# First layer of a four-layer kernel: the skip term and gate as five VectorE operations, and GpSimd's fading ahead of its scatters and fetches

## What is computed

```python
xBC = causal_conv_silu(xBC, conv_w)            # xs (512), B (128), C (128)
dt  = softplus(dt_raw + dt_bias); cum = cumsum(dt * A) in each chunk
Yd   = sum over j <= i of (C_i . B_j) * exp(cum_i - cum_j) * dt_j * xs_j
Yoff = exp(cum_i) * C_i . S_before             # S: the state before the chunk
S    = exp(cum_last) * S + sum of wdec * B * xs
y    = Yd + Yoff + D * xs                      # D * xs: the skip term
yz   = y * silu(z)                             # the gate
out  = (yz * rsqrt(mean(yz * yz) + eps) * norm_w) @ W_out.T
```

## Time and profile before

| | us |
|---|---|
| median of 3 runs | 1502.84 |
| lowest, highest | 1494.15, 1506.90 |
| the profiled execution, own time | 1498.83 |
| its span (first to last instruction) | 1497.1 |
| chunk loops of the first layer end, and the second layer starts, about | 587 |

### The profile page before, as it was taken

The page is one execution under the profiler, slowest core; times in us unless marked ns, Lnnn a source line. Parts: engine busy times, 40 slices in busy tenths (PEclk is TensorE's granted clock), DMA queues, the critical chain, the costliest instruction groups (busy, mean ns, idle before and its releaser), DMA issues. The chain is left out here.

```text
span 1497.1 us, 21861 instructions
## 1 busy us (share of the span) xinstructions
PE 1286.0 (86%) x7439; PEld 804.8 (54%) x7443; DVE 885.9 (59%) x1723; ACT 567.9 (38%) x957; POOL 354.7 (24%) x344
## 2 busy tenths in 40 slices
PE   5677988998988687999999998999766989998987
PEld 3334646654664455666666644454543456544564
DVE  5767566556656585543224379889777453556334
ACT  2474476547647551222222242443312313223311
POOL 3186031221302522510301002221037000000045
PEclk9788999999999888999999999999857999999999
DMA  9142123122211412300000150000002100111123
GB/s 360 55 139 84 47 60 96 50 54 71 79 41 35 132 51 97 103 1 0 0 0 0 68 186 0 1 0 1 2 28 85 31 28 29 36 43 57 57 58 111
DMA packets 72082, 88.87 MB, mean 59 GB/s; under 512 B 19174, under 2 KB 55334, under 8 KB 71337
## 3 DMA queue, kind: packets, MB, share of 16 engines
q1 hardware_dynamic: 65836, 70.78, 15.1%
q0 software_dynamic: 6144, 16.79, 3.5%
HBM read 61.14 MB, written 26.38 MB: 58 GB/s over the span
## 5 line engine op out<-in xcount | busy, mean ns | idle before, releaser
L414 PE MATMUL l_banks<-l_xnT,all_region_a 128*128 128x512 f32 x288 | 133.7, 612 | 5.6 <-ACTq L805 4.8
L2019 PE MATMUL l_banks<-l_xnT,mid_region_c 128*128 128x512 f32 (+1 forms) x192 | 89.6, 617 | 10.8 <-DVE l_xnT L2235 10.8
L970 POOL TENSOR_TENSOR all_region_b<-all_region_b,l_lc 128x512 f32<-128x512 f32 x64 | 88.2, 1398 | 31.5 <-DMA all_region_b<-l_lc_rows 31.2
L414 PEld LDWEIGHTS l_banks<-l_xnT,all_region_a 128*128 128x128 f32 x288 | 55.0, 197 | 65.9 <-issue 55.5
L794 ACT ACTIVATE all_region_b<-all_region_b 128x512 f32<-128x512 f32 x64 | 69.5, 1087 | 17.9 <-PE l_banks L414 14.0
L414 PE MATMUL l_banks<-all_region_a,all_xa 128*128 x234 | 68.7, 411 | 6.9 <-DVE all_x L1041 5.4
L1200 DVE SCALAR_TENSOR_TENSOR l_xbc<-l_pre,all_cols,l_xbc 128x512 f32<-128x512 f32 x72 | 61.7, 857 | 19.2 <-ACT l_xbc L727 14.2
L2019 PEld LDWEIGHTS l_banks<-l_xnT,mid_region_c 128*128 128x128 f32 (+1 forms) x192 | 35.2, 189 | 57.3 <-issue 45.4
L962 POOL TENSOR_TENSOR l_yr<-l_yr,all_neg_half 128x1 f32<-128x1 f32 x16 | 10.3, 643 | 232.7 <-DVE l_yr L1063 232.7
L2902 POOL TENSOR_TENSOR l_rstd<-l_moments,all_neg_half 128x4 f32<-128x4 f32 x12 | 12.4, 1032 | 220.8 <-DVE l_moments L2962 220.8
L1257 DVE TENSOR_TENSOR all_region_b<-all_region_b,l_cbd 128x512 f32<-128x512 f32 x64 | 59.0, 924 | 7.6 <-ACT all_region_b L794 3.9
(11 more groups left out here) (475 smaller groups left out, 2854.6 us busy)
## 6 DMA issues: line engine op xcount, KB each, us to landing
all_region_b<-l_lc_rows SPq DMA_DIRECT2D x256, 64.0 KB, 2.0
all_xa<-slots_in SPq DMA_DIRECT2D x39, 128.0 KB, 2.1
slots_out<-all_xa SPq DMA_DIRECT2D x39, 128.0 KB, 2.1
mid_vector_rows<-slots_in SPq DMA_DIRECT2D x39, 128.0 KB, 2.1
slots_out<-all_region_a SPq DMA_DIRECT2D x39, 128.0 KB, 1.7
slots_in<-l_xp SPq DMA_DIRECT2D x4, 1024.0 KB, 12.8
all_region_a<-l_gate_up SPq DMA_DIRECT2D x1, 4096.0 KB, 15.8
all_x<-x SPq DMA_DIRECT2D x4, 512.0 KB, 5.7
```

The lines of the kernel that those rows point to most:

```text
L414: return nc.tensor.matmul(out, lhsT, rhs, start=start, stop=stop, **kw)
L970: nc.gpsimd.tensor_tensor(bc[:, k, :, :], bc[:, k, :, :], spread(lc[:, c, heads], 1, BLK), ALU.subtract).then_inc(dd_ready.sem, 1)
L2019: return nc.tensor.matmul(out, lhsT, rhs, start=start, stop=stop)
```

## The change

The skip matmuls and their diagonal matrix are gone. `assemble` starts the sum in PSUM itself. VectorE's `take_y` forms y + D * xs by four operations of 128 columns (one input in SBUF, one in PSUM, D as a scalar for each partition), waits for them, and gates by a fifth of 512 columns with both inputs in SBUF. ScalarE waits for it before it overwrites `xbc` for the next group. GpSimd's list and loop are new, and three places where VectorE adds the fetched rows and measures.

```diff
         def assemble(g, c):
+            pe.wait_ge(yd_ready.sem, yd_ready.done(g, c))
+            jobs.wait_room(pe, 0, ("y", g, c))
             bank = jobs.bank(("y", g, c))
-            pe.wait_ge(yd_ready.sem, yd_ready.done(g, c))
...
-                    mm(yout[32 * m:32 * m + 32, :, q, :], turn[:, q, :], yd[:, m::4, :], False, False,
+                    mm(yout[32 * m:32 * m + 32, :, q, :], turn[:, q, :], yd[:, m::4, :], q == 0, False,
...
-        def skipped(g, c):
...
-                mm(bank[:, k * P:(k + 1) * P], skip[:, k, :], xbc[:, k, c * P:(c + 1) * P], k == 0, False,
-                   skip_group_check=True)
...
-                    if k == 1:
-                        skipped(g, c)
                     near(g, c, k)
...
                 if j == 0 and g > 0:
                     act.wait_ge(conv_ready.sem, conv_ready.done(g - 1))
+                    act.wait_ge(yg_ready.sem, yg_ready.done(g - 1))
...
-            skips(g)
...
-        late = {0: ((6,), (7, 8)), 1: ((9, 10), (11, 12)), 2: ((13, 14, 15), ())}
+        late = {0: ((4,), (5, 6, 7)), 1: ((), (8, 9, 10, 11)), 2: ((), (12, 13, 14, 15))}
...
             differences(g, 0)
-            if g == 0:
-                for t in range(GT, GT + 2):
-                    scatter(t)
             for c in range(NCH):
+                fade(g, c)
+                ahead, behind = late.get(c, ((), ())) if g == 0 else ((), ())
+                for t in ahead:
+                    scatter(t)
+                if c + 1 < NCH:
+                    differences(g, c + 1)
+                for t in behind:
+                    scatter(t)
                 if (g, c) == (GROUPS - 1, 1):
                     for t in range(GT):
                         fetch(t)
-                fade(g, c)
...
                 if c > 0:
                     out_scale(g, c - 1)
-                for t in behind:
-                    scatter(t)
...
-            nc.vector.tensor_tensor(yg[:, :, :], jobs.bank(("y", g, c)).rearrange("p (k n) -> p k n", k=Z_BLK),
-                                    zs[:, :, c * P:(c + 1) * P], ALU.mult).then_inc(yg_ready.sem, 1)
+            bank = jobs.bank(("y", g, c))
+            for k in range(Z_BLK):
+                nc.vector.scalar_tensor_tensor(
+                    out=yg[:, k, :], in0=xbc[:, k, c * P:(c + 1) * P], scalar=col("D", k),
+                    in1=bank[:, k * P:(k + 1) * P], op0=ALU.mult, op1=ALU.add)
             jobs.free(dve.drain(), ("y", g, c))
+            nc.vector.tensor_tensor(yg[:, :, :], yg[:, :, :], zs[:, :, c * P:(c + 1) * P], ALU.mult).then_inc(
+                yg_ready.sem, 1)
...
                 tiles_and_unit(g, c, 1)
-                if (g, c) == (GROUPS - 1, 1):
-                    add(0)
-                    add(1)
+                if (g, c) == (GROUPS - 1, 2):
+                    add(2)
+                    add(3)
...
                 tiles_and_unit(g, c, 2)
-                if (g, c) == (GROUPS - 1, 1):
-                    add(2)
-                    add(3)
+                if (g, c) == (GROUPS - 1, 2):
+                    measure(0)
...
                     out_stats(g, c - 1)
                 if (g, c) == (GROUPS - 1, 1):
-                    measure(0)
+                    add(0)
+                    add(1)
```

More of the change, by code:

```diff
@@ L174, in layer0 @@
     yr = sb("yr", [P, 2])
-    skip = pre[:, 4, CONV_K - 1:].rearrange("p (k n) -> p k n", k=Z_BLK)
     lmax = sb("lmax", [P, TILES])
@@ L304, in layer0 @@
     yd_ready = Event(sem("l0_yd_ready"), NCH)
-    skip_ready = Event(sem("l0_skip_ready"), 1)
     yg_ready = Event(sem("l0_yg_ready"), NCH)
@@ L587, in assemble @@
             jobs.fill(last, ("y", g, c))
-        def skipped(g, c):
-            if c == 0:
-                pe.wait_ge(skip_ready.sem, skip_ready.done(g))
-            jobs.wait_room(pe, 0, ("y", g, c))
-            bank = jobs.bank(("y", g, c))
-            for k in range(Z_BLK):
-                mm(bank[:, k * P:(k + 1) * P], skip[:, k, :], xbc[:, k, c * P:(c + 1) * P], k == 0, False,
-                   skip_group_check=True)
         def out_proj(g, c):
@@ L766, in conv_silu @@
             nc.scalar.activation(xbc[:, j, :], xbc[:, j, :], ACT.Silu).then_inc(xbc_ready.sem, 1)
-        def skips(g):
-            act.wait_ge(conv_ready.sem, conv_ready.done(g, 4))
-            if g == 0:
-                act.wait_ge(mem.const_ready, mem.n_const)
-            for k in range(Z_BLK):
-                last = nc.scalar.activation(skip[:, k, :], ident[:, :], ACT.Copy, scale=col("D", k))
-            last.then_inc(skip_ready.sem, 1)
         def place(g, c):
@@ L1009, in _ @@
             differences(g, 0)
-            if g == 0:
-                for t in range(GT, GT + 2):
+            for c in range(NCH):
+                fade(g, c)
+                ahead, behind = late.get(c, ((), ())) if g == 0 else ((), ())
+                for t in ahead:
                     scatter(t)
-            for c in range(NCH):
+                if c + 1 < NCH:
+                    differences(g, c + 1)
+                for t in behind:
+                    scatter(t)
                 if (g, c) == (GROUPS - 1, 1):
@@ L1016, in _ @@
                         fetch(t)
-                fade(g, c)
-                ahead, behind = late.get(c, ((), ())) if g == 0 else ((), ())
-                if c + 1 < NCH:
-                    differences(g, c + 1)
-                    for t in ahead:
-                        scatter(t)
                 if c > 0:
                     out_scale(g, c - 1)
-                for t in behind:
-                    scatter(t)
                 if (g, c) == (GROUPS - 1, 2):
```

## The result

The changed kernel takes 1507.2 us (median of 20 runs, 1502.15 to 1512.31); the kernel before, run beside it, takes 1497.95 us (20 runs, 1494.15 to 1506.9). The ratio on record is 1.0052, 95% interval 1.0039 to 1.0064 (the two medians alone give 1.0062): slower, by less than one per cent but by more than chance. The forecast was 1488 us, range 1472 to 1506. The profiled execution has a span of 1503.1 us against 1497.1. The first layer's last chunk hands over to the second layer 3.9 us later, the rest of the program, which is the same code, takes 2.1 us longer. Such a difference says little: over the thirteen profiled executions of this case that rest took between 906.8 and 915.6 us. From here on a chunk runs from one `take_y` to the next, as in the prediction, where nothing else is said.

A forecast was written before the change was run, and what follows sets the result against it. TensorE, busy for 86%, was seen waiting for VectorE, its longest waits leading to GpSimd. Terms 2.6 - 0.8 - 3.5 - 16.9 + 5.4 + 1.2 = -12.0 us gave 1486.8 (1490.8 from the median); forecast 1488, range 1472 to 1506.

The forecast's parts named there:

- Price of the new `take_y`: VectorE, per `take_y`: four operations 1.1 us, gate issued at 1.25, masking of piece 1 done at 5.45; +1.7 us.
- Chunks with tiles: Ten chunks with expert tiles: 1.06 us of matmuls go from each, but the longer `take_y` outweighs it; sum +2.6 us.
- rival (c): Gate held through the fade and four differences, masking 4.1 us later in each of seven chunks: +29, 1516 us; chance 0.12.
- (0, 2) to (0, 3), -3.5 us: Group 0: earlier fade shortens (0, 2), but normalising waits for eight scatters; 4.3 us gained, 0.8 lost to `take_y`.
- (3, 1), -16.9 us: Fade ahead of the fetches ends masking at 511.05 instead of 521.84; adds and measuring move out: -16.9 us.
- (3, 2), +5.4 us: Masking 1.9 us later, one pair of `add` and the measuring come in, small waits go: 26.9 us, +5.4.
- (3, 3) and the tail: (3, 3): bank freed 1.05 us later, skip matmuls gone: 0; layer's end: longer `take_y` in a row of work: +1.2 us.
- ScalarE's copies: Four ScalarE copies at L774 go, some 1.3 us a group: -0.2 us for each group, -0.8 in all.
- the new wait for `yg`: ScalarE's first copy moves by 0.2 us at three group starts, where it waits for TensorE anyway: 0.
- Rival (b): VectorE sets the pace; the 1.7 us pass whole seven times: 11.9 instead of 2.6, 1496 us; chance 0.15.

The follow-up runs named there:

- skip half alone: The changed kernel with GpSimd's order and VectorE's adds and statistics put back as before the change: 1514.79 us, ratio 1.0086 to the kernel before.
- both remedies: The changed kernel with "far" in bank 2 instead of 1 and the gate issued behind `from_state`: 1492.09 us, ratio 0.9948 to the kernel before.
- order-alone kernel: The kernel before with only GpSimd's new order and VectorE's moved adds and statistics, skip term still on TensorE: 1485.24 us, ratio 0.9902.

## Why the prediction was wrong

By its own steps, with the starts of `take_y` in the two profiled executions:

- **Price of the new `take_y`: right.** 1.12 us for 1.1, gate issued at 1.24 for 1.25, masking done at 5.45 as said. The gate took 1.28 or 1.29 us beside a fade in most chunks. The four new operations took 1.12 us also at 534.20, where the fade ran beside them from 534.16.
- **Chunks with tiles, +2.6 us: the step that failed.** The six chunks of groups 1 and 2 that have a `take_y` came out at +1.3, -0.3, +0.4, +1.3, +1.2 and +4.5, together +8.4, where the steps gave +2.6. Each was walked through from `near` on ("TensorE reaches `near` at 382.0 instead of 383.0"). But TensorE comes to `near` only through `far`, and `far` needs the bank that `from_state` frees. In (2, 1) it waited there 1.53 us, so TensorE came no earlier to `near`, and `dn` and the rest behind it moved with it. The prediction knew that bank, but counted it only for (3, 3). In (2, 3) the granted clock also fell to 0.87, from 1.00 before. This term was off by 5.8 us, more than any other; the same wait at `far`, which has no term anywhere in the sum, is also in (0, 3), (3, 2) and (3, 3) below.
- **(0, 1), no term: missed.** 2.6 us longer, the hold of 5.99 us. That is rival (c), in one chunk and not in seven; the 29 us it was priced at didn't come.
- **(0, 2) to (0, 3), -3.5 us: half right.** (0, 2) is 3.0 us shorter and its normalising waits 4.04 us for the scatters, as forecast. But (0, 3) is 1.5 longer, again by `far`: 5.59 us. The step has a slip of its own: eight scatters of 1.23 us from 135.8 end at 145.6, not 146.1. They took longer, too: 11.5 us from the first to the end of the last (138.18 to 149.63).
- **(3, 1), -16.9 us: right, a little too large:** -15.1. Mechanism confirmed by the kernels with and without the fade ahead.
- **(3, 2), +5.4 us: undersized:** +7.5, with 2.75 us at `far` and a clock of 0.82.
- **(3, 3) and the tail, 0 and +1.2:** +2.8 and +1.2. "The bank that `from_state` frees comes 1.05 later and the skip matmuls go: 0" fell on its second half: those matmuls come behind `far`, so that their going can't repay a wait ahead of it, and the wait grew from 3.42 to 4.43.
- **ScalarE's copies, -0.8, and the new wait for `yg`, 0:** the three group starts came out at -1.0, -0.8 and +0.3.

These differences and -0.5 us at the start add up to +3.9 us at the end of the first layer. The prediction had -12.0 there. Seen from the profiled execution, 1486.8 us were forecast and 1504.9 measured: 15.9 us of the miss are these, 2.1 the layers that were not touched. Rival (b) had the right direction for the tile chunks but, for most of it, the wrong reason: with the same work on VectorE, one operation moved or one bank changed took back 12 to 14 us. Its bound of +11.9 for seven chunks still left the total below before, since the rest of the gains was kept. The measured 1507.2 lies just above the range because no rival delayed `far`. The rule of the Trainium skill that was quoted (SBUF — State Buffer, Who interferes with whom) would, as the prediction took it, end the hold of the gate with the one operation that was under way. The row of 5.99 us goes through five, so for this row the measurement decides against that reading; with the 1.29 us of (2, 1) it agrees.

## What to carry to other kernels

An operation that gets longer delays not only what reads its result but every buffer that is freed behind it on its engine: list, for the operations behind it in that queue, which bank or semaphore each frees, and who takes that next, before walking through any chunk. An operation that only makes a result for later (here the gate) belongs behind the one that frees a shared bank, or the two users get banks of their own. The effects of two edits that touch the same wait can't simply be added: removing a long wait can uncover what was hidden beneath it.

## What was not expected of the hardware

- The hold of a VectorE operation with two SBUF inputs came in two forms. Where GpSimd's fade followed its indirect DMAs without a rest, it lasted through all of the differences: 5.99 us in the changed kernel, 5.98 with the skip half alone, 4.56 before, 5.85 with both remedies (there with the short `out_scale` between DMAs and fade). Where GpSimd had rested, the gates and maskings of (2, 1) and (3, 1) took 1.29 to 1.31. In the kernel with the gate later GpSimd had rested 1.93 us ahead of the fade of (0, 1), and the gate took 1.71. GpSimd's side differs with it: in the changed kernel the four differences took 4.91 us in (0, 1), where VectorE was held, and 5.88 to 5.90 in (0, 2), (2, 1) and (3, 1), where it was let in. That the rest makes the difference was not tried by itself, and one row speaks against it: in (3, 2) of the order-alone kernel the fade came without a rest behind `out_scale` and the fetches, and the masking took 1.52.
- 17.8 us of matmuls less on TensorE, in a stretch in which it was busy for 86%, brought no time. Its busy time fell by only 2.5 us and the granted clock from 0.97 to 0.95. How much of this is the clock and how much the way in which busy time is counted stays open. With `take_y` made longer the other side shows: the same 4047 matmuls took 404.0 us of busy time instead of 393.8, again at 0.95 instead of 0.97.
